# One PSUM bank moved from the shared products to the row maxima in a fused attention and expert kernel

## What is computed

```
h = concat(x[t], x[t+3], x[t+6]) @ W.T + b                 # "tok"
n = layernorm(h)
q, k, v = n @ Wq.T, n @ Wk.T, n @ Wv.T                     # "qk", "v"
att = softmax(where(causal, q @ k.T / 4, -inf))
h = h + (att @ v) @ Wp.T + bp                              # "proj"
n = layernorm(h)
logits = n @ wr + br; two best experts with softmax gates
out = h + sum over the chosen e of gate * (gelu(n @ w1[e] + b1[e]) @ w2[e] + b2[e]) + terms of the constants
```

## Time and profile before

| | |
|---|---|
| time before, median of 3 runs | 1868.71 us (1864.55 to 1869.48) |
| the profiled execution | 1868.96 us |
| its span | 1867.2 us |
| mean granted clock of PE | 0.901 |
| PE busy | 1551.3 us (83%) |
| DVE busy | 1097.4 us (59%) |
| POOL busy | 835.7 us (45%) |
| ACT busy | 709.6 us (38%) |

### The profile page before, as it was taken

The page is one execution under the profiler, slowest core; times in us unless marked ns, Lnnn a source line. Parts: engine busy times, 40 slices in busy tenths (PEclk is TensorE's granted clock), DMA queues, the critical chain, the costliest instruction groups (busy, mean ns, idle before and its releaser), DMA issues.

```text
span 1867.2 us, 33109 instructions
## 1 busy us (share of the span) xinstructions
PE 1551.3 (83%) x10648; PEld 1196.2 (64%) x10648; DVE 1097.4 (59%) x3458; ACT 709.6 (38%) x1463; POOL 835.7 (45%) x912
## 2 busy tenths in 40 slices
PE   2679798798798698698797787459999999999997
PEld 2536474474374374374464442459999999999997
DVE  1366668667577577577577580335555555555554
ACT  0114544444444444444434554023333333333332
POOL 4313334544634535536436335224444444545444
PEclk9759998898897798899898896779999999999999
DMA  3251633733724624625526457354545555554551
GB/s 93 70 108 41 169 85 103 194 85 99 193 63 127 164 73 138 150 68 155 137 69 170 104 163 214 96 169 157 198 163 186 181 177 184 169 197 152 192 175 62
DMA packets 166971, 256.23 MB, mean 137 GB/s; under 512 B 30484, under 2 KB 97998, under 8 KB 166800
## 3 DMA queue, kind: packets, MB, share of 16 engines
q1 hardware_dynamic: 108816, 166.66, 31.2%
q10 hardware_dynamic: 34368, 50.33, 9.1%
q0 software_dynamic: 23616, 37.12, 6.7%
HBM read 173.92 MB, written 75.29 MB: 133 GB/s over the span
## 4 chain that ended last, share of the span: by engine, by line
PE 53%; issue 14%; DVE 10%; DMA 9%; POOL 8%; ACT 3%; SPq 2%; ACTq 0%; DVEq 0%; POOLq 0%
PE yb L1383 14%; PE l1b L1370 13%; PE pab L1094 8%; PE pvb L1194 6%; DMA qk_s<-parts 5%; PE mxb L1154 4%; PE stb L1171 4%; POOL xs L674 4%; DVE unused L898 2%; PE rb L1341 1%; DMA r_s<-invs 1%; POOL prob L685 1%; DMA invb<-r_s 1%; PE pab L1136 1%; ACT hf L1254 1%
## 5 line engine op out<-in xcount | busy, mean ns | idle before, releaser
L760 ACT ACTIVATE prob<-stb 124x496 f32<-124x496 f32 (+2 forms) x832 | 401.7, 505 | 464.2 <-PE stb L1171 426.9
L898 DVE CUSTOM_DVE_ANT_0 unused<-mxb,mask_row 124x372 bf16<-124x372 f32 (+4 forms) x768 | 352.7, 484 | 84.9 <-PE mxb L1154 80.8
L1154 PE MATMUL mxb<-kst,qst 96*124 96x372 bf16 (+4 forms) x1024 | 321.2, 345 | 80.7 <-DVE mxp L898 47.8
L1171 PE MATMUL stb<-qst,kst 99*124 99x372 bf16 (+4 forms) x1024 | 316.9, 344 | 65.2 <-DMA qst<-negp 42.7
L1383 PE MATMUL yb<-w2p,hp 128*128 x2448 | 339.4, 284 | 10.1 <-DVE yo L1325 10.1
L1370 PE MATMUL l1b<-x2T,w1s 128*128 128x384 f32 x1632 | 336.5, 341 | 1.2 <-DVE x2T L1284 1.2
L1383 PEld LDWEIGHTS yb<-w2p,hp 128*128 128x128 f32 x2448 | 323.7, 189 | 20.5 <-issue 20.5
L1254 ACT ACTIVATE hf<-l1b,b1c 128x384 f32<-128x384 f32 x272 | 158.3, 582 | 340.5 <-PE l1b L1370 301.6
L1370 PEld LDWEIGHTS l1b<-x2T,w1s 128*128 128x128 f32 x1632 | 275.4, 189 | 1.6 <-DVE x2T L1284 1.6
L1171 PEld LDWEIGHTS stb<-qst,kst 99*124 99x124 bf16 x1024 | 138.8, 145 | 197.7 <-ACT prob L760 79.7
L1154 PEld LDWEIGHTS mxb<-kst,qst 96*124 96x124 bf16 x1024 | 141.3, 146 | 177.9 <-DVE mxp L898 94.8
(11 more groups left out here) (158 smaller groups left out, 1543.8 us busy)
## 6 DMA issues: line engine op xcount, KB each, us to landing
w1s<-ws SPq DMA_DIRECT2D x34, 2048.0 KB, 8.4
qk_s<-parts SPq DMA_DIRECT2D x64, 279.0 KB
xg<-xs SPq DMA_DIRECT2D x34, 396.0 KB
kst<-qk_s SPq DMA_DIRECT2D x32, 279.0 KB, 3.8
qst<-qk_s SPq DMA_DIRECT2D x32, 279.0 KB, 6.4
wraw<-in_w_all ACTq DMA_DIRECT2D x32, 256.0 KB
ws<-whi ACTq DMA_DIRECT2D x32, 256.0 KB
ws<-wlo ACTq DMA_DIRECT2D x32, 256.0 KB
```

The lines of the kernel that those rows point to most:

```text
L760: act.activation(dst, src, ACT.Exp, scale=DH ** -0.5).then_inc(exp_done, 1)
L898: done = dve.tensor_tensor_reduce(out=unused[:, n % 2, e * w:(e + 1) * w], in0=src, in1=mask_row[:, T - w:T], scale=1.0, scalar=-3.0e38, o ...
L1154: done = nc.tensor.matmul(out, qst[g % NG][0:ROWS, h + e, TT * i:TT * i + TT], kst[g % NG][0:ROWS, h + e, k0:k0 + w], start=True, stop=True)
L1171: done = nc.tensor.matmul(out, kst[g][:, h, TT * j:TT * j + TT], qst[g][:, h, q0:q0 + w], start=True, stop=True)
```

## The change

The number of banks for the maxima, `MXB`, goes from 2 to 3, and the number of banks for the shared products, `PAB`, from 2 to 1. `STB` stays 2. PSUM has eight banks here before and after: 2 + 2 + 2 (`pvb`) + 2, and 3 + 2 + 2 + 1. No instruction is added, taken away or moved in its engine's order. What changes is the bank that each product writes and the counts in the waits of line 1151 and of `take_bank`: a piece of maxima waits for the third before it in place of the second, and a shared product waits until the one just before it has been read.

```
--- before.py
+++ after.py
@@ -53,7 +53,7 @@
       + [[(3, h, 3 * TT, 3 * TT), (5, h, 5 * TT, TT)] for h in range(HG)]
       + [[(4, h, 4 * TT, 2 * TT), (4, h + 1, 4 * TT, 2 * TT)] for h in (0, 2)])
 NMX, NST = len(MX), len(ST)
-MXB, STB, PAB = 2, 2, 2
+MXB, STB, PAB = 3, 2, 1
 assert (NG * NMX) % MXB == 0 and (NG * NST) % STB == 0
 
 PV_ORDER = (0, 1, 2, 3, 5, 4)
```

## The result

The changed kernel takes 1934.25 us (median of 4 runs, 1930.23 to 1940.44) against 1869.1 us before; the ratio is 1.035, with a 95% interval of 1.032 to 1.039. The execution profiled took 1930.48 us with a span of 1928.7 us, 61.5 us more than the span before. The forecast was 1910 us with a range of 1882 to 1945: the direction and the range held, the size was short by 24 us.

The account below looks back on a forecast made before the run. PE, DVE and transfers were taken to set the pace in different stretches. Middle batches 21, first 3, last 2, front 5, tail 2.5 and clock 7 us sum to 40.5 us, giving 1910 us, range 1882 to 1945.

Parts of the forecast that it names:

- v and tok: Products in each middle batch waiting for the shared bank's reader while PE is full: 2.9 us and 2.0 us lost.
- proj and turn: Shared-bank products in a middle batch where DVE sets the pace: 1.5 us lost, between 0.5 and 4.7.
- The third bank: Extra bank for the maxima lets PE run further ahead of DVE: gives back 3.4 us per batch, between 1 and 7.
- six middle batches: Attention batches between first and last: 6 x (6.9 - 3.4) = 21 us lost, between 0 and 45.
- Front: Before the batches: tok loses 2.4 us, turns 3.5, maxima regain 0.9; 5.0 us lost in sum.
- Tail: Six proj products at the end, each now followed by its reader: 2.5 us lost.
- Clock in the batches: New pauses lower PE's clock once more in every third of seven batches: 7 us, bounds 0 and 41.
- Rival B: PE's clock falls in each batch, in v and in tok: 41 us in place of 7, 1944 us; chance 0.20.
- front and first batch: The part before the batches, 5.0 us lost, and the first batch, which has no proj, about 3 us lost.
- Rival C: Third bank pays: batches gain 25 us, front and tail lose 7.5, giving 1851 us; chance 0.07 for faster.
- D: Batch gains and losses even out, or transfers hide more: 1863 to 1876 us; chance 0.08.
- the period: Sign in the profile: a middle batch grows from 134.9 to about 139 us; no growth would refute the prediction.

Follow-up runs that it names:

- filled tail of the changed kernel: The changed kernel with 33 matmuls that nobody reads, made by PE while it waits before the tail's six proj products; 1939.78 us, ratio 1.035.

## Why the prediction was right in direction and short in size

**v and tok: right.** The forecast was 2.9 + 2.0 us a middle batch; the aligned traces give 3.1 + 1.9 us on the mean of batches 1 to 6, and the run with the spare bank there took back 41 us in all, the 42 us that these losses sum to.

**proj and turn: right for the shared bank.** They were to cost 1.5 us, and 0.9 after the third bank's share. The delay grows by 1.5 us from the last tok to the first qk on the mean (0.3 to 3.0), and by 1.3 us without the third bank: the bank's share isn't there.

**The third bank: the step that failed.** "3.4 us per batch, between 1 and 7". From the first qk of a batch to the first v of the next the delay should have shrunk by 2 us or more and grows by 0.7; without the third bank by 0.6. The waits for DVE did shrink, as the prediction said, by 26 us in the sum, and between the fourth and the last qk PE did gain 2.8 us where 2.3 were booked. The error was to let that gain move everything behind it. The prediction had written that the store sets the pace in the first part of qk and booked nothing there, but had no store in the second part; in the batch that it read, ACT waited for PE there and not for the store. The runs show that a PE which is earlier by the third bank meets the store at the last qk, in each of the six batches, and hands the whole gain back before the next batch. Moving the qk two slots earlier met the same stores. This is some 22 us in the six middle batches, 43.2 us where 21 were forecast. In the front the third bank does pay, some 2 us against 0.9 forecast.

**Front: right in sum, wrong in its parts.** 5.6 us against 5.0. A pause in tok costs 0.77 us and not 0.48: the reader and the release were counted, but before, a product of 2.4 us was followed by the next after 2.15 to 2.19 us, so that the record of its last matmul still ran while the next product began. That overlap of some 0.25 us (the drain, in what follows) is lost too. The v pairs were taken from start and end and held this. The turns cost 4.3 us and not 3.5. Against 2.4 us more lost, 1.8 us more came back than booked: 2.7 us from the first qk to the first v, of which 0.7 come back without the third bank as well.

**Tail: a term that was mis-sized.** 2.5 us forecast, 7.4 measured. The five pauses of 0.52 us are 2.6 us of it, as forecast. The rest, 4.9 us, is that the six products take 2.09 us each, 12.6 us in all and not 7.70: the drain again, and the clock, which before came to the upper level within the run and now stays at the lower one from first to last. In the filled tail of the changed kernel the upper level was lost in the second product, in that of the kernel before, without the pauses, it lasted through all six.

**Clock in the batches: a term of 7 us that isn't there.** The granted clock from 127 us to the tail's start is 0.89 after and 0.88 before, and v and tok run at 1.00. Rival B is wrong for the batches and right for the tail. Its 7 us covered by luck a part of what the third bank didn't give: the terms missed by +22 us (middle batches), +5 (tail), +1 (front and first batch) and -7 (clock), which gives the 21 us between the 40.5 us forecast and the 61.5 us of the profiled execution.

**Rival C**, the third bank pays for all, is refuted by the result and by the run without that bank; **D**, all hidden, by the period: 141.9 us a middle batch on the mean after, 134.7 us before.

**Open:** the length of one batch scatters by several microseconds between batches of the same kernel (139.9 to 144.0 us), with the transfers. Batch 3 gained 5 us behind its qk, and did so without the third bank too; it is the long one in the trace before (138.3 us), while the kernel before with 20 unread matmuls in the tail has 135.7 us there, so that the gain is at least in part an accident of the trace before. Why batch 2 lost 4 us (1 us without the third bank) isn't settled. That the stores alone hold back the third bank's gain is read from three traces of it and one without, not from a run with faster stores or a fourth buffer.

## What to carry to other kernels

A bank shared in turn is worth what its reader takes at the moment when the writer is full: count, for each pair of neighbours, the end of the reader against the start of the next product, add the drain of the last matmul, and add up only where the writer has no other wait nearby. A wait that shrinks is no gain until the next wait of the whole chain has been looked at, that of the readers included: here the writer came 2.8 us earlier and the reader's own output buffer, still being stored, took it all back. The second buffer of a pair bought 366 us here (a fallen clock among them) and the third at most some 8. Where an engine with a throttled clock waits for microseconds and then does work on the path, unread work up to the end of the wait can be cheaper than the wait.

## What the runs showed of the hardware beyond expectation

Twenty unread matmuls that ended 6 us before the work left the first product as slow as none (2.10 us); thirty-three that ended 1.7 us before it made it 1.14 us. In that run the clock fell from the upper level to the lower behind a wait of 1.67 us, one product of 1.14 us and a pause of 0.52 us, and stayed there through the pauses of 0.52 us that followed (1.14, 1.58, 2.09 us for the same product), while in the batches pauses of 0.2 to 0.3 us for ACT in every 1.5 us left it at 1.00. The Trainium skill, page "TensorE: Matmul & The Clock Gate", section "A second HAM failure mode: psum-queue depth-cycling", describes small idles between groups of matmuls, from cycling through banks, that make the clock swing between its levels. The batches don't bear this out for pauses of that size; in the tail longer ones went with the lower clock, which stayed there and didn't swing.
